# First attention of a four-stage kernel: score matmuls on 32 rows at the row group of their head, two heads on a pair of PSUM banks

## The reference

```python
qkv = (h @ w_qkv + b_qkv).reshape(B, T, 3, NUM_HEADS, HEAD_DIM)   # B 4, T 1024, 16 heads of 8
scores = jnp.einsum('bhqd,bhkd->bhqk', q, k) / np.sqrt(HEAD_DIM)
attn = jax.nn.softmax(scores, axis=-1)
out = jnp.einsum('bhqk,bhkd->bhqd', attn, v)
```

## Time and profile before

| | us |
|---|---|
| median of 3 runs | 3062.42 |
| lowest and highest | 3059.94, 3063.07 |
| profiled execution | 3059.87 |
| its span | 3058.1 |

### The profile page before, as it was taken

The page is one execution under the profiler, slowest core; times in us unless marked ns, Lnnn a source line. Parts: engine busy times, 40 slices in busy tenths (PEclk is TensorE's granted clock), DMA queues, the critical chain, the costliest instruction groups (busy, mean ns, idle before and its releaser), DMA issues.

```text
span 3058.1 us, 46676 instructions
## 1 busy us (share of the span) xinstructions
PE 2868.1 (94%) x16447; PEld 2218.5 (73%) x16447; DVE 2592.4 (85%) x4498; ACT 2055.2 (67%) x4414; POOL 1704.2 (56%) x1188
## 2 busy tenths in 40 slices
PE   6999999999999999999998998999899999999896
PEld 3555555555547777787887887888788888888785
DVE  8888888887868787788889889889889989988987
ACT  3777777776775555776676676676677677677673
POOL 5421513322105555676677676786677677667763
PEclk9999999999999999999999999999999999999998
DMA  1000000000022121000000000000000000000000
GB/s 46 15 9 8 15 8 15 8 11 13 8 78 80 49 78 56 8 1 1 1 1 3 3 1 3 3 1 3 3 1 3 3 1 3 3 2 2 3 3 6
DMA packets 28569, 42.69 MB, mean 14 GB/s; under 512 B 5097, under 2 KB 15913, under 8 KB 28337
## 3 DMA queue, kind: packets, MB, share of 16 engines
q1 hardware_dynamic: 28336, 39.72, 4.4%
...
## 4 chain that ended last, share of the span: by engine, by line
PE 62%; DVE 24%; issue 10%; POOL 2%; ACT 2%; SPq 0%; DMA 0%; DVEq 0%; POOLq 0%
PE P L1820 12%; PE P L1661 8%; PE P L1688 8%; PE P L1673 8%; DVE c_nm L1390 7%; PE P L1847 6%; DVE c_DT L1415 5%; PE P L1749 4%; PE P L1831 4%; DVE xres L1451 3%; PE P L1857 2%; PE P L1803 2%; PE P L1760 2%; PE P L1647 2%; DVE d_tc L1495 1%
## 5 line engine op out<-in xcount | busy, mean ns | idle before, releaser
L911 ACT ACTIVATE c_P<-P,c_nm 128x1024 f32<-128x1024 f32 x512 | 571.9, 1117 | 349.9 <-DVE c_nm L1390 345.9
L1390 DVE TENSOR_REDUCE c_nm<-P 128x1 f32<-128x1024 f32 x512 | 622.5, 1216 | 173.7 <-PE P L1820 173.0
L1214 DVE TENSOR_REDUCE a_mx<-P 128x1 f32<-128x512 f32 x1024 | 641.4, 682 | 120.1 <-PE P L1661 119.4
L787 ACT ACTIVATE a_PT<-P 128x512 f32<-128x512 f32 x1024 | 531.6, 601 | 162.2 <-PE P L1673 160.9
L2058 POOL TENSOR_TENSOR c_P<-c_P,c_P 128x1024 f32<-128x1024 f32 (+1 forms) x256 | 615.8, 2405 | 21.4
L2056 POOL TENSOR_SCALAR c_P<-c_P,c_rr 128x1024 f32<-128x1024 f32 (+1 forms) x256 | 301.5, 1178 | 475.7 <-DVE c_rr L1402 475.6
L1847 PE MATMUL P<-c_DT,c_xkh 128*128 128x256 f32 x2048 | 462.1, 288 | 24.0 <-DVE c_Yl L1423 21.1
L1661 PE MATMUL P<-a_Kp,a_Qs 128*128 128x512 f32 x1024 | 427.4, 422 | 12.8 <-DVE a_mx L1214 5.8
L1673 PE MATMUL P<-a_Qs,a_Kp 128*128 128x512 f32 x1024 | 401.2, 395 | 3.0 <-ACT a_PT L787 1.4
L1847 PEld LDWEIGHTS P<-c_DT,c_xkh 128*128 128x128 f32 x2048 | 355.0, 191 | 32.1 <-DVE c_Yl L1423 26.9
L1820 PE MATMUL P<-c_xth,c_Th 128*128 128x512 f32 x1024 | 367.4, 440 | 2.9 <-ACT c_P L911 2.9
...
## 6 DMA issues: line engine op xcount, KB each, us to landing
...
a_Qs<-a_mT SPq DMA_DIRECT2D x256, 2.0 KB
...
```

The costliest lines, as they stand in the source:

```text
L787: e.activation(m.PT[j][hs % 4][:, :], bank("scores", u, hs, j), ACT.Exp, scale=SCALE).then_inc(m.S["a_exp"])
L911: e.activation(m.P1[s][n % 4][:, :], P[:, k:k + 2, :].rearrange("p c k -> p (c k)"), ACT.Exp, bias=m.nm[:, n % 4, s:s + 1], accum_out=m.sm ...
L1214: e.tensor_reduce(m.mx2[u % 2][:, 16 * (t // 4) + 4 * j + t % 4, half:half + 1], bank("maxima", u, t, j, half), AX, ALU.max).then_inc(m.S[ ...
L1390: e.tensor_reduce(m.nm[:, n % 4, s:s + 1], P[:, k:k + 2, :].rearrange("p c k -> p (c k)"), AX, ALU.max, negate=True).then_inc(m.S["c_nm"])
```

## The change

- The keys of a unit stand once, in `Ks[u % 3]`, [128, 1024], as the queries do. `Kp`, `Kc`, the zeroing and the four key DMAs of a unit are gone; GpSimd writes `Ks` directly, and for the first unit VectorE alone does so.
- A `maxima` or `scores` step is now for two heads (`two` = 0 or 1): two matmuls of 32 rows each, at partitions 32j, into two neighbouring banks, and the second alone signals. VectorE reduces both banks in one instruction (out 128x2), ScalarE exponentiates both in one (128x1024) into `PT`, now [128, 2, 512].
- `maxima` and `scores` take their banks from one ring of three pairs, (0, 1), (2, 3), (5, 6); all hooked steps use bank 7. In a step of 8 slots the even ones hold a `maxima` pair, the odd ones a `scores` pair, so the amount of work per step is the same; `sums` stays in slots 1 and 5, behind the `scores` of the slot.
- Hooked steps have moved: `values` to slot 7 (from 3), `row2` to 5 (from 2), `divide` to 4, `turn_o` to 7 and `out_project` to 5 (from 1).

The diff, cut to what the prediction speaks of:

```diff
-    ring = Ring([3, 5, 6, 7])
-    st_ring = Ring([0, 1, 2])
+    ring = Ring([7, 0, 2, 5])
+    twos = Ring([(0, 1), (2, 3), (5, 6)])
...
+    ring.slots = [7]
...
-                hook(s0 + 19 + c, 3, "values", b + 1, c)
+                hook(s0 + 19 + c, 7, "values", b + 1, c)
...
-            hook(s0 + 4 + 4 * c, 2, "row2", u, c)
+            hook(s0 + 4 + 4 * c, 5, "row2", u, c)
         e0 = s0 + LAG0
         for r in range(2):
-            hook(e0 + 5 + 4 * r, 1, "divide", u, r)
+            hook(e0 + 5 + 4 * r, 4, "divide", u, r)
             if gr == 3:
-                hook(e0 + 6 + 4 * r, 1, "turn_o", b, r)
-                hook(e0 + 7 + 4 * r, 1, "out_project", b, r)
+                hook(e0 + 6 + 4 * r, 7, "turn_o", b, r)
+                hook(e0 + 7 + 4 * r, 5, "out_project", b, r)
...
-            um, m = divmod(8 * s + i, 64)
-            ue, m_e = divmod(8 * (s - LAG0) + i, 64)
-            up, m_p = divmod(8 * (s - LAG0 - 1) + i, 64)
-            if um == 0 and m < 32:
-                on_ring("maxima", 0, m // 4 % 4, m % 4, m // 16)
-            elif um < NU:
-                on_ring("maxima", um, m // 8, m // 2 % 4, m % 2)
-            if 0 <= ue < NU:
-                p.on([st_ring.take()], "scores", ue, m_e // 4, m_e % 4)
+            um, m = divmod(2 * s + i // 4, 16)
+            ue, m_e = divmod(2 * (s - LAG0) + i // 4, 16)
+            up, m_p = divmod(2 * (s - LAG0 - 1) + i // 4, 16)
+            if i % 2 == 0 and um < NU:
+                t, half = (m % 4, m // 4) if um == 0 and m < 8 else (m // 2, m % 2)
+                p.on(twos.take(), "maxima", um, t, half, i // 2 % 2)
+            if i % 2 and 0 <= ue < NU:
+                p.on(twos.take(), "scores", ue, m_e, i // 2 % 2)
             if i % 4 == 1 and 0 <= up < NU:
-                if m_p // 4 == 0:
-                    p.on([4], "sums", up, m_p // 4)
+                if m_p == 0:
+                    p.on([4], "sums", up, m_p)
                 else:
-                    p.do("sums", up, m_p // 4)
+                    p.do("sums", up, m_p)
...
-    def scores(u, hs, j):
-        w.wait_ge(*at("a_st", "scores", u, hs, j))
+    def scores(u, hs, two):
+        k = v.plan.bank["scores", u, hs, two]
+        w.wait_ge(*at("a_st", "scores", u, hs, two))
         if 16 * u + hs > 3:
             w.wait_ge(*at("a_pv", "sums", *divmod(16 * u + hs - 4, 16)))
-        e.activation(m.PT[j][hs % 4][:, :], bank("scores", u, hs, j), ACT.Exp, scale=SCALE).then_inc(m.S["a_exp"])
+        e.activation(m.PT[two][hs % 4][:, :, :].rearrange("p j q -> p (j q)"),
+                     P[:, k:k + 2, :].rearrange("p j q -> p (j q)"), ACT.Exp, scale=SCALE).then_inc(m.S["a_exp"])
...
-        if wh:
-            w.wait_ge(*v.now("a_z", "project", u, wh, c))
-            for j in range(2):
-                r = slice(32 * j, 32 * j + 32)
-                e.tensor_tensor(m.Kp[0][r, j, cs], m.th[q][r, :], m.tq[q][r, :], ALU.add).then_inc(s)
-        else:
-            e.tensor_tensor(m.Qs[0][:, cs], m.th[q][:, :], m.tq[q][:, :], ALU.add).then_inc(s)
+        e.tensor_tensor((m.Ks if wh else m.Qs)[0][:, cs], m.th[q][:, :], m.tq[q][:, :], ALU.add).then_inc(s)
...
-    def maxima(u, t, j, half):
-        w.wait_ge(*at("a_max_pe", "maxima", u, t, j, half))
+    def maxima(u, t, half, two):
+        k = v.plan.bank["maxima", u, t, half, two]
+        w.wait_ge(*at("a_max_pe", "maxima", u, t, half, two))
         if u > 1:
             w.wait_ge(*at("a_nm", "row1", u - 2, t // 4))
-        e.tensor_reduce(m.mx2[u % 2][:, 16 * (t // 4) + 4 * j + t % 4, half:half + 1], bank("maxima", u, t, j, half),
+        e.tensor_reduce(m.mx2[u % 2][:, t // 4, 2 * two:2 * two + 2, t % 4, half], P[:, k:k + 2, :],
                         AX, ALU.max).then_inc(m.S["a_max_dve"])
...
-    def maxima(u, t, j, half):
-        ps = bank("maxima", u, t, j, half)
+    def maxima(u, t, half, two):
+        bank("maxima", u, t, half, two)
+        k = v.plan.bank["maxima", u, t, half, two]
         if u == 0:
-
-            if j > 1:
-                w.wait_ge(*at("a_qs", "project", 0, 1, half, i=j - 1))
-            else:
-                w.wait_ge(*at("a_first_dve", "project", 0, 1, half, i=3 + j))
+            w.wait_ge(*at("a_first_dve", "project", 0, 1, half))
         else:
-            w.wait_ge(*at(f"a_kdma{u % 3}", "project", u, 1, 1))
+            w.wait_ge(*at("a_qs", "project", u, 1, half))
         w.wait_ge(*at("a_first_dve" if u == 0 and t < 4 else "a_qs", "project", u, 0, t // 4))
-        e.matmul(ps, m.Qs[u % 3][:, 128 * t:128 * t + 128], m.Kp[u % 3][:, j, 512 * half:512 * half + 512],
-                 start=True, stop=True).then_inc(m.S["a_max_pe"])
+        for j in (2 * two, 2 * two + 1):
+            r = slice(32 * j, 32 * j + 32)
+            tt = e.matmul(P[:, k + j % 2, :], m.Qs[u % 3][r, 128 * t:128 * t + 128],
+                          m.Ks[u % 3][r, 512 * half:512 * half + 512], start=True, stop=True)
+        tt.then_inc(m.S["a_max_pe"])
...
-    def scores(u, hs, j):
+    def scores(u, hs, two):
         c, kt = divmod(hs, 8)
-        ps = bank("scores", u, hs, j)
+        bank("scores", u, hs, two)
+        k = v.plan.bank["scores", u, hs, two]
         w.wait_ge(*at(f"a_mdma{u % 3}_{c}", "row2_low", u, c))
-        e.matmul(ps, m.Kp[u % 3][:, j, 128 * kt:128 * kt + 128], m.Qs[u % 3][:, 512 * c:512 * c + 512],
-                 start=True, stop=True).then_inc(m.S["a_st"])
+        for j in (2 * two, 2 * two + 1):
+            r = slice(32 * j, 32 * j + 32)
+            tt = e.matmul(P[:, k + j % 2, :], m.Ks[u % 3][r, 128 * kt:128 * kt + 128],
+                          m.Qs[u % 3][r, 512 * c:512 * c + 512], start=True, stop=True)
+        tt.then_inc(m.S["a_st"])
...
-        if (u, wh) == (0, 1):
-            w.wait_ge(*at("a_first_dve", "project", u, wh, c, i=2))
-            w.wait_ge(*v.now("a_z", "project", u, wh, c))
-            for j in range(2, 4):
-                r = slice(32 * j, 32 * j + 32)
-                e.tensor_tensor(m.Kp[0][r, j, cs], m.th[q][r, :], m.tq[q][r, :], ALU.add).then_inc(m.S["a_qs"])
-        elif (u, c) != (0, 0):
+        if u or (wh, c) == (0, 1):
             w.wait_ge(*at("a_tq", "project", u, wh, c))
             e.tensor_scalar(m.th[q][:, :].bitcast(F32R), m.tq[q][:, :], 1.0, 0.0, ALU.mult,
                             ALU.add).then_inc(m.S["a_th"])
@@ -2026,11 +2006,9 @@
             e.tensor_scalar(m.th[q][:, :], m.th[q][:, :], m.msk[:, wh:wh + 1], 0.0, ALU.mult,
                             ALU.add).then_inc(m.S["a_th"])
             w.wait_ge(*at("a_th", "project", u, wh, c))
-            if wh == 0 and u > 2:
-                w.wait_ge(*at("a_st", "scores", u - 3, 15, 3))
-            if wh and u > 2:
-                w.wait_ge(*at(f"a_kdma{(u - 2) % 3}", "project", u - 2, 1, 1))
-            dst = m.Kc[u % 2] if wh else m.Qs[u % 3]
+            if u > 2:
+                w.wait_ge(*at("a_st", "scores", u - 3, 15, 1))
+            dst = m.Ks[u % 3] if wh else m.Qs[u % 3]
...
-    def project(u, wh, c):
-        if u and wh and c:
-            w.wait_ge(*at("a_qs", "project", u, 1, 1))
-            w.wait_ge(*at("a_z", "zero", u % 3))
-            if u > 2:
-                w.wait_ge(*at("a_st", "scores", u - 3, 15, 3))
-            for j in range(4):
-                e.dma_start(m.Kp[u % 3][32 * j:32 * j + 32, j, :].bitcast(F32),
-                            m.Kc[u % 2][32 * j:32 * j + 32, :].bitcast(F32)).then_inc(S[f"a_kdma{u % 3}"], 16)
```

More of the change, by code:

```diff
@@ L136, in project_signals @@
     out = {"a_qk_pe": 1, "a_tq": 1}
-    if u == 0 and w == 1:
-        out |= {"a_first_dve": 4, "a_qs": 2}
-    elif u == 0 and c == 0:
+    if u == 0 and (w == 1 or c == 0):
         out |= {"a_first_dve": 3}
@@ L142, in project_signals @@
         out |= {"a_th": 2, "a_qs": 1}
-    if u and w and c:
-        out[f"a_kdma{u % 3}"] = 64
     return out
@@ L155 @@
 SIGNALS = {
-    "zero": {"a_z": 1},
     "one": {"a_z": 1},
@@ L558, in memory @@
     free_from = top
-    m.Kp, m.Qs = [None] * 3, [None] * 3
+    m.Ks, m.Qs = [None] * 3, [None] * 3
     for i in (1, 2):
-        m.Kp[i] = sb(f"a_Kp{i}", [128, 4, T], F32R)
+        m.Ks[i] = sb(f"a_Ks{i}", [128, T], F32R)
         m.Qs[i] = sb(f"a_Qs{i}", [128, T], F32R)
-    m.Kc = [sb(f"a_Kc{i}", [128, T], F32R) for i in range(2)]
     m.hT = sb("a_hT", [128, T])
@@ L573, in memory @@
     m.wv = sb("a_wv", [128, 128])
-    assert top == A_EARLY, top
-    m.Kp[0] = sb("a_Kp0", [128, 4, T], F32R)
+    assert top <= A_EARLY, top
+    top = A_EARLY
+    m.Ks[0] = sb("a_Ks0", [128, T], F32R)
     m.Qs[0] = sb("a_Qs0", [128, T], F32R)
-    m.PT = [[sb(f"a_PT{j}_{i}", [128, 512]) for i in range(4)] for j in range(4)]
+    m.PT = [[sb(f"a_PT{j}_{i}", [128, 2, 512]) for i in range(4)] for j in range(2)]
     m.Vp = [sb(f"a_Vp{i}", [128, NT * 144 + 32]) for i in range(2)]
@@ L588, in memory @@
     m.bvo = sb("a_bvo", [128, 2, 128])
-    m.mx2 = [sb(f"a_mx{i}", [128, 32, 2]) for i in range(2)]
```

(22 more changed lines are left out.)

9 lines of the change are left out of this document (2 added, 7 removed).

## The result

| | before | after |
|---|---|---|
| median | 3061.86 us | 3171.05 us |
| lowest and highest | 3059.94, 3063.07 | 3156.09, 3177.51 |
| profiled execution | 3059.9 (span 3058.1) | 3177.1 (span 3175.3) |

The ratio is 1.035, 95% interval 1.031 to 1.039: the change makes the kernel slower by 109 us of median. The forecast was 42 us slower. The sign and the loop were right; the size was less than half of what came.

A forecast was written before the change was run, and what follows sets the result against it. TensorE's own work was taken to set the pace, 3.04 us per half-step; a new 3.30 us loop would replace it. Steady stretch +50, start -4, end -4: +42 on 3059.9, so 3102 us, range 3050 to 3205 us.

The forecast's parts named there:

- The loop: First attention, each half-step (four slots): reduce, score pair, `sums`, maxima pair, reduce in a ring; 3.30 us against 3.04 before.
- d: How much later the second matmul of a pair ends; taken as 0.03 us, counted twice in the loop's 3.24 + 2d.
- the rival's 3.70 us: Loop length per half-step if a pair's two matmuls run in line, d = 0.23; 3200 us in all, chance 0.13.
- M0' and S0': Next half-step's first maxima pair and first scores pair; TensorE was to idle about 0.9 us between them.
- The guests: Other steps hooked into the first attention's slots (`project`, `divide`, `row2` and so on): 57 us in place of 71.
- steady stretch: First score to last maximum, 244 half-steps with both scores and maxima: 862 us against 812, +50 us.
- The clock: Rival: TensorE's clock falls to the 1.2 GHz level because it idles more; above 3250 us, chance 0.04.
- The ends: Outside the steady stretch: start -4 us, first maximum 3.4 us sooner; end -4 us, with 0 to 8 as bounds.
- row DMAs: 8 DMAs per half unit bring row maxima to the queries; no cost in the steady stretch, about 1 us wait at first scores.
- the pair in line: Rival: row groups bring nothing, d = 0.23, loop 3.70 us, 98 us more, 3200 us; chance 0.13.
- The likeliest case: The loop as forecast: 3070 to 3145 us, d from 0 to 0.11, loop terms by 0.05 us either way; chance 0.68.
- The short matmul: Rival: a 32-row matmul's latency shrinks with its rows, the loop loses 2 x 0.20 us, 3004 us; chance 0.10.

The follow-up runs named there:

- e5: The changed kernel with VectorE's maxima reading only 256 of each 512 score columns; 3049.48 us, ratio to before 0.995.
- e2: The changed kernel with keys zero-padded again and matmuls over all 128 rows, bank pairs and rings kept; 3209.46 us, ratio to before 1.048.
- e4: The changed kernel with the first maxima pair of each half-step issued three times, same result; 3131.52 us, ratio to before 1.023.
- e7: The changed kernel with padded keys and 128-row matmuls, VectorE reading each second maxima pair twice; 3491.73 us, ratio to before 1.140.
- e8: The kernel before with keys stored once, 32-row matmuls, single banks and old rings, guests moved to the slots of the scores; 2997.51 us, ratio to before 0.978.
- e3: The kernel before with keys stored once and 32-row matmuls at their row groups, single banks and old rings kept; 3024.87 us, ratio to before 0.988.

## Why the prediction was right and wrong

**The loop: right.** 3.30 us forecast, 3.25 measured. d was taken as 0.03 and is 0.01 or less; the reduce is 1220 ns for 1216; reading and start terms held. e5 moved one term and the half-step followed to 0.01 us, e2 gave the rival's 3.70 us with its own condition (128 rows, in line). TensorE idles 1.10 us between M0' and S0', forecast 0.9.

**The guests: too small.** At full clock the steady stretch is 920.6 - 55 = 866 us, +54 where +50 was forecast. But 244 x 3.25 is 793, so guests and stalls are 73 us and not 57; the too long loop (12 us) hid most of that. One part is the single bank 7 of all hooked steps, which the forecast had not priced, as the timeline of TensorE shows: the `turn_o` transposes wait for ScalarE to read what `turn_h` left there.

```profile
425.61 0.66 PE L1613 MATMUL P<-ident,a_hn 128*128 128x128 f32 x4
...
428.13 0.66 PE L1685 MATMUL P<-ident,a_OT 128*128 128x128 f32 x4 [1.44 <-ACT a_hT L749]
```

Such a wait occurs three times only (3.1 us); the rest I did not separate.

**The clock: the step that failed.** The forecast gave it 0.04, by "gaps of 0.9 us between bursts speak against it", and thought of the clock as either full or low throughout. In the trace after it goes back and forth, a fifth of the stage at the lower level, and that costs 55 us: the greater part of the 75 us that were missing on the profiled execution (117 for 42; the others are the steady stretch at full clock with 4, the end with 13, start and rest with 3). The trace of before could not show it: it has neither a 32-row matmul nor a gap in the half-step, and its low clock in the first 50 us, where TensorE is busy half the time, was the only hint. The argument from the gaps was no evidence, since no row had gaps of that kind at full clock. That it is the clock is shown: e4 leaves the loop at 3.25 us, has 0.98 and is 40 us faster. Why the clock falls is shown in part only: not with 128 rows (e2, e7), and with 32 rows not only where the gaps are long (e8).

Before the fall at about 429 us the timeline has gaps of 1.1 us in each half-step and then 1.44 us for `turn_o`; before that at 570 us, gaps of 1.25 and 1.09 us. The Trainium skill, TensorE: Matmul & The Clock Gate, section "A second HAM failure mode: psum-queue depth-cycling", tells of a kernel in which short idle times between groups of matmuls, from cycling through PSUM, let the clock go up and down. The trace after has both, such idle times and a clock that goes up and down (0.91); I had not weighed that section. It does not tell e7, whose gaps are longer and whose clock is 0.99, from the changed kernel.

**The ends.** The start was right in size, the first score 2.8 us sooner (forecast 4), but not by its steps. The first maximum, forecast 3.4 us sooner, starts at 24.8 us in both kernels: the forecast laid VectorE's slow steps there to the padded write, but without that write the mask step took 3.47 us where it took 0.49 before (at 17.53), while GpSimd ran adds on `xres`. And the first scores waited 3.2 us for their row DMAs, not 1. The timelines of VectorE and TensorE:

```profile
18.03 3.47 DVE L1188 TENSOR_SCALAR a_th<-a_th,a_msk 128x512 f32<-128x512 f32 x1
...
57.65 0.79 PE L1661 MATMUL P<-a_Qs,a_Ks 32*128 32x512 f32 x2 [3.16 <-DMA a_Qs<-a_mT]
```

The second key half saved its 1.7 us as forecast (0.69 us at 29.16 for 2.35). That the sum came out near is in part luck. At the end the forecast was 4 us of gain; it became 9.3 us of loss. The forecast had priced the wait for the row DMAs in the steady stretch, where two half-steps of 3.3 us are ahead of it, and at the start, but not here. In the last half-steps `sums` starts at 980.38, 982.11 and 984.19, 1.7 to 2.1 us apart; `row2` stands three slots later, and VectorE's subtract ahead of the DMAs came at 985.32, 2.5 us after ScalarE had written the row (982.56 + 0.25), behind VectorE's work for the second stage. The DMAs took the same 4.9 us as before (875.62 there) and the score waited 6.0 us. Behind that wait the clock is low again: `sums` takes 1.94 us at 992.42.

**The range** held the time (3050 to 3205), but not for a reason that it was made for: its upper end was the pair in line, which is refuted (d = 0.01). The likeliest case's own range, 3070 to 3145, holds the time at full clock (3177 - 55 = 3122) and not the measured one.

**The short matmul** fell: a single 32-row matmul that had waited lasts 0.49 us (e3, 326.17), where one of 128 rows takes 0.50, and `sums` starts 0.42 us after the waiting score.
